# Two Mamba layers: delta spread by DMA, and centring, skip and residual as matmuls

## What is computed

```python
def _mamba_block(seq, ...):                      # seq (b, L, 96), L = 4096
    mu = seq.mean(-1, keepdims=True)
    var = ((seq - mu) ** 2).mean(-1, keepdims=True)
    h = (seq - mu) * jax.lax.rsqrt(var + EPS) * ln_g + ln_b
    xz = h @ in_w
    xs, z = jnp.split(xz, 2, axis=-1)            # 192 channels each
    xp = jnp.pad(xs, ((0, 0), (DCONV - 1, 0), (0, 0)))
    xc = sum((conv_w[:, k] * xp[:, k:k + L, :] for k in range(DCONV))) + conv_b
    xc = jax.nn.silu(xc)
    dbl = xc @ xproj_w                           # dt (6), Bm (16), Cm (16)
    delta = jax.nn.softplus(dt @ dt_w + dt_b)
    dA = jnp.exp(delta[..., None] * A)
    dBx = delta[..., None] * Bm[:, :, None, :] * xc[..., None]
    hstates = scan over L of h = dA * h + dBx    # 16 states per channel
    y = jnp.einsum('blds,bls->bld', hstates, Cm) + Dp * xc
    y = y * jax.nn.silu(z)
    return y @ out_w
seq = seq + _mamba_block(seq, ...)               # twice
```

## Time and profile before

| | |
|---|---|
| median of three runs | 9348.97 us |
| the profiled execution | 9345.01 us, span from first to last instruction 9342.9 us |
| PE (TensorE) busy | 7302.2 us, 78% |
| DVE (VectorE) | 6834.6 us, 73% |
| POOL (GpSimd) | 5443.5 us, 58% |
| ACT (ScalarE) | 4997.8 us, 53% |
| granted TensorE clock, mean | 0.857 of full |
| DMA, all on SyncE's hardware queue | 698 MB, 30.7% of 16 engines' span |

### The profile page before, as it was taken

How to read it: one execution, slowest core, us unless ns; L and a number is a source line. 1 busy time by engine, 2 the same in 40 slices (tenths; PEclk the granted TensorE clock), 3 DMA queues, 4 the chain that set the end, 5 groups by cost and what they waited for, 6 DMA issues and landing times. The chain is left out here.

```text
span 9342.9 us, 107667 instructions
## 1 busy us (share of the span) xinstructions
PE 7302.2 (78%) x19376; PEld 2489.5 (27%) x19376; DVE 6834.6 (73%) x7955; ACT 4997.8 (53%) x10430; POOL 5443.5 (58%) x4360
## 2 busy tenths in 40 slices
PE   7777777767777777288888888788888886888877
PEld 2222222222222222022222222222222221445433
DVE  6877878858878788558888899388888895532445
ACT  5555555545555555345566666455666664321456
POOL 5666666656666666147777778377777784000325
PEclk8888888878888888689999999889999998996688
DMA  2222222212222222423333343233333343165322
GB/s 52 48 47 47 47 47 47 46 42 49 51 49 51 48 48 45 118 70 79 83 85 85 85 92 86 59 81 82 89 89 89 91 95 82 78 210 162 100 55 76
DMA packets 367705, 698.09 MB, mean 75 GB/s; under 512 B 41415, under 2 KB 109372, under 8 KB 362364
## 3 DMA queue, kind: packets, MB, share of 16 engines
q1 hardware_dynamic: 367420, 695.26, 30.7%
HBM read 568.49 MB, written 126.63 MB: 74 GB/s over the span
## 5 line engine op out<-in xcount | busy, mean ns | idle before, releaser
L591 POOL TENSOR_TENSOR mamba_prod<-mamba_hs,mamba_BC_rep 128x512 f32<-128x512 f32 x1536 | 1935.1, 1267 | 1123.5 <-DVE mamba_hs L533 1113.6
L533 DVE TENSOR_TENSOR_SCAN mamba_hs<-mamba_dA,mamba_carry,mamba_dbx 128x512 f32<-128x512 f32 x1152 | 1464.4, 1271 | 130.1 <-ACT mamba_dA L462 123.4
L462 ACT ACTIVATE mamba_dA<-mamba_delta_rep,mamba_a_neg 128x512 f32<-128x512 f32 x1536 | 1036.9, 679 | 846.7 <-PE mamba_delta_rep L293 795.7
L1539 POOL TENSOR_TENSOR scan_a_prod<-scan_a_hs,scan_a_BC_rep 128x512 f32<-128x512 f32 x768 | 979.2, 1275 | 479.5 <-DVE scan_a_hs L1465 381.6
L1539 POOL TENSOR_TENSOR scan_b_prod<-scan_b_hs,scan_b_BC_rep 128x512 f32<-128x512 f32 x768 | 979.3, 1275 | 469.0 <-DVE scan_b_hs L1465 373.4
L293 PE MATMUL mamba_delta_rep<-mamba_du,mamba_sel 96*128 96x512 f32 x768 | 529.8, 778 | 653.4 <-ACT mamba_dA L462 653.3
L507 DVE TENSOR_TENSOR mamba_dbx<-mamba_u_rep,mamba_BC_rep 128x512 f32<-128x512 f32 x1152 | 790.2, 686 | 111.5 <-PE mamba_u_rep L293 56.9
L1846 POOL TENSOR_TENSOR ffn_sq<-ffn_xm 96x512 f32<-96x512 f32 x64 | 66.2, 1035 | 1156.5 <-DVE ffn_xm L1814 1145.7
L293 PE MATMUL mamba_u_rep<-mamba_du,mamba_sel 96*128 96x512 f32 x768 | 494.3, 731 | 234.8 <-DVE mamba_hs L533 155.4
L256 PE MATMUL mamba_pre<-mamba_h,mamba_w_conv 96*96 96x512 f32 x1024 | 611.0, 719 | 18.7 <-POOL mamba_tails L561 13.4
L1311 ACT ACTIVATE scan_a_dA<-scan_a_delta_rep,scan_a_a_neg 128x512 f32<-128x512 f32 x768 | 518.4, 678 | 156.7 <-PE scan_a_delta_rep L1098 143.5
(11 more groups left out here) (365 smaller groups left out, 14212.3 us busy)
## 6 DMA issues: line engine op xcount, KB each, us to landing
mamba_BC_rep<-bc_units SPq DMA_DIRECT2D x256, 512.0 KB, 9.4
scan_a_BC_rep<-bc_rows SPq DMA_DIRECT2D x512, 256.0 KB, 5.0
scan_b_BC_rep<-bc_rows SPq DMA_DIRECT2D x512, 256.0 KB, 4.8
by_n<-fin_res SPq DMA_DIRECT2D x32, 768.0 KB, 3.3
fmid_src<-by_n SPq DMA_DIRECT2D x32, 768.0 KB, 6.2
by_k<-fmid_res SPq DMA_DIRECT2D x32, 768.0 KB, 4.3
fout_src<-by_k SPq DMA_DIRECT2D x32, 768.0 KB, 4.7
seq<-mamba_xo SPq DMA_DIRECT2D x64, 192.0 KB, 2.1
```

What stands on the lines that cost most here:

```text
L462: nc.scalar.activation(dA[:, s % RING_A], delta_rep[:], ACT.Exp, scale=a_neg[:, s:s + 1]).then_inc(s_dA, 1)
L533: nc.vector.tensor_tensor_scan(hs[:, s % RING_H], dA[:, s % RING_A], dbx_bank(s)[:], carry[:, bass.ds(at, 1)], op0=ALU.mult, op1=ALU.add). ...
L591: pool.tensor_tensor(prod[:, (G * u + s) % RING_P], hs[:, s % RING_H], BC_rep[:, u, QUADS + s % QUADS], ALU.mult).then_inc(s_prod, 1)
L1539: pool.tensor_tensor(prod[:, (G * k + s) % RING_P], hs[:, (G * k + s) % RING_H], BC_rep[:, k, 2 + s % 2], ALU.mult).then_inc(s_prod, 1)
```

## The change

Delta is no longer spread by matmuls: each softplus half of 96 x 512 is stored to HBM (`delta_rows`), and read back in four loads of 192 KB (32 partitions x 3 blocks x 512 tokens) into `delta_rep`, now a tile in SBUF for two units (`spread_delta`, called for half 0 and half 1 ahead of `spread_bc` on SyncE's queue). dA waits for it in steps 0 and 12. The bank that this frees takes the output sum `out_ps`. Centring is one matmul with (identity - 1/96); ScalarE copies the result (`xm`) and squares it. The skip is a matmul of xc with a diagonal matrix that opens the sums in `y`, the residual one with the identity that opens `out_ps`; ScalarE evicts `out_ps` in its step 14 (`evict_out`). The gate moves from GpSimd to VectorE and reads `y` in PSUM; it stands where `add_skip` stood. Further: RING_H 6 to 8, RING_A 4 to 6, the projection in steps 10 and 11, softplus in ScalarE's steps 15 to 17, `copy_bc` in step 17 (was 12), `add_softplus` in steps 13 and 14, `project_out` in steps 7 and 8, buffers reused in place, softplus's halves with semaphores of their own.

The diff, with declarations, setup and context cut:

```diff
-    RING_H = 6
-    RING_A = 4
+    RING_H = 8
+    RING_A = 6
...
-        sp_abs = p.sb("sp_abs", [C, 2, T])
-        sp_exp = p.sb("sp_exp", [C, 2, T])
...
-        du = p.sb("du", [C, 2, 2, 2, T])
+        delta = p.sb("delta", [C, 2, T])
+        du = p.sb("du", [C, 2, 2, T])
+        delta_rep = p.sb("delta_rep", [128, 2, BLOCKS, T])
...
-        dA = p.sb("dA", [128, 4, T])
+        dA = p.sb("dA", [128, RING_A, T])
...
-        yg = p.sb("yg", [C, 2, T])
...
-        delta_rep = p.ps("delta_rep")
+        out_ps = p.ps("out_ps", (C, T))
...
+            def spread_delta(v, half, done, landed):
+
+                sp.wait_ge(s_delta[half], done)
+                sp.dma_start(delta_rows[v, half], delta[:, half]).then_inc(s_delta_out[half], 16)
+                sp.wait_ge(s_delta_out[half], landed)
+                by_block = delta_rows[v, half].rearrange("(b c) t -> c b t", c=32)
+                for k in range(NB):
+                    sp.dma_start(delta_rep[32 * k:32 * k + 32, v, HB * half:HB * half + HB], by_block
+                                 ).then_inc(s_rep_d[half], 16)
...
             def body(n, u, has_next, has_ahead):
...
                 if not (isinstance(n, int) and n + 3 >= UNITS):
-                    wait(sp, s_xm, read)
...
                                  ).then_inc(s_xin[1 - u], 16)
-                wait(sp, s_xo, last)
+                wait(sp, s_out, last)
...
+                    spread_delta(1 - u, 0, done, landed)
+                    spread_delta(1 - u, 1, done, landed)
...
-            sp.wait_ge(s_xm, 1)
...
+            spread_delta(0, 0, 1, 16)
+            spread_delta(0, 1, 1, 16)
...
+            pe.wait_ge(s_diag, 3)
...
             def mean(m, v):
...
-                nc.tensor.matmul(pre[0][0:C], mean_w[:], xin[:, v], start=True, stop=True).then_inc(s_mean, 1)
+                nc.tensor.matmul(pre[0][0:C], centre_w[:], xin[:, v], start=True, stop=True).then_inc(s_mean, 1)
...
             def project(m, v, half, has_ahead=False):
...
-                if half == 0:
-                    wait(pe, s_xo, m - 1)
-                elif has_ahead:
+                if half and has_ahead:
...
-            def project_out(n, kh):
-                if kh == 0 and isinstance(n, int) and n == UNITS - 1:
-                    pe.wait_ge(s_xo, n)
-                elif kh == 0 and isinstance(n, int) and n == UNITS - 2:
-                    pe.wait_ge(s_relu, 2 * n + 3)
-                elif kh == 0:
-                    pe.wait_ge(s_raw, 4 * n + 11)
+            def project_out(n, u, kh):
+                if kh == 0:
+                    wait(pe, s_xo, n)
+                    pe.wait_ge(s_xres[u], 16 * (n // 2 + 1) if isinstance(n, int) else 8 * (n - u) + 16)
+                    nc.tensor.matmul(out_ps[:], ident[:], xres[:, u], start=True, stop=False)
                 pe.wait_ge(s_yg, 2 * n + kh + 1)
-                mm = nc.tensor.matmul(pre[1][0:C], w_out[:, kh], yg[:, kh], start=(kh == 0), stop=(kh == 1))
+                mm = nc.tensor.matmul(out_ps[:], w_out[:, kh], ysk[:, kh], start=False, stop=(kh == 1))
...
-            def replicate(bank, v, what, b):
-
-                return nc.tensor.matmul(bank[:], sel[:, b % HB], du[:, v, what, b // HB], start=True, stop=True)
-
-            def rep_delta(v, b):
-                replicate(delta_rep, v, 0, b).then_inc(s_rep_d, 1)
...
             def rep_input(v, b):
-                replicate(u_rep[b % 2], v, 1, b).then_inc(s_rep_u, 1)
+                nc.tensor.matmul(u_rep[b % 2][:], sel[:, b % HB], du[:, v, b // HB], start=True, stop=True
+                                 ).then_inc(s_rep_u, 1)
...
             def sum_quad(n, u, half, i):
...
                 if i == 0:
-                    wait(pe, s_ysk, 2 * n + half)
+                    wait(pe, s_yg, 2 * n + half)
+                    nc.tensor.matmul(y[:], skip_w[:, half], xc[:, u, half], start=True, stop=False)
...
                                             prod[:, (G * u + HG * half + QUADS * c + i) % RING_P],
-                                            start=(i == 0), stop=(i == QUADS - 1))
+                                            start=False, stop=(i == QUADS - 1))
...
             def next_step(s, m, v, has_ahead):
-                if 8 <= s < 10:
-                    project(m, v, s - 8, has_ahead)
+                if 10 <= s < 12:
+                    project(m, v, s - 10, has_ahead)
...
             def ahead_step(s, m, v):
-                if s == 1:
+                if s == 2:
                     mean(m, v)
-                elif s == 5:
+                elif s == 6:
...
             def body(n, u, has_next, has_ahead):
                 for s in range(G):
                     b = s // QUADS
-                    if s % QUADS == 1 and (b + 1 < BLOCKS or has_next):
-                        if b + 1 == BLOCKS:
-                            pe.wait_ge(s_du, 3 * n + 5)
-                        pe.wait_ge(s_dA, G * n + QUADS * (b + 1))
-                        rep_delta(u if b + 1 < BLOCKS else 1 - u, (b + 1) % BLOCKS)
...
                         if b + 2 == BLOCKS:
-                            pe.wait_ge(s_du, 3 * n + 6)
+                            pe.wait_ge(s_du, n + 2)
...
                         next_step(s, n + 1, 1 - u, has_ahead)
-                    if s in (4, 6) and not (isinstance(n, int) and n == 0):
-                        project_out(n - 1, (s - 4) // 2)
+                    if s in (7, 8) and not (isinstance(n, int) and n == 0):
+                        project_out(n - 1, 1 - u, s - 7)
...
+            for half in range(2):
+                nc.scalar.activation(skip_w[:, half], ident[:], ACT.Copy, scale=skip[:, half:half + 1]).then_inc(s_diag, 1)
...
             def rsqrt(m):
...
-                nc.scalar.activation(lnv[:], pre[0][0:C], ACT.Ln, bias=eps[:]).then_inc(s_ln, 1)
+                wait(act, s_xh, m)
+                nc.scalar.activation(rstd[:], pre[0][0:C], ACT.Ln, bias=eps[:]).then_inc(s_ln, 1)
...
-                wait(act, s_xh, m)
-                nc.scalar.activation(rstd[:], lnv[:], ACT.Exp, scale=-0.5).then_inc(s_rstd, 1)
+                nc.scalar.activation(rstd[:], rstd[:], ACT.Exp, scale=-0.5).then_inc(s_rstd, 1)
...
             def softplus_begin(m, half):
...
-                wait(act, s_du, 3 * m)
-                nc.scalar.activation(sp_abs[:, half], pre[1 - half][0:C], ACT.Abs, bias=dt_b[:, half:half + 1]
+                wait(act, s_delta[half], m)
+                nc.scalar.activation(sp_ln[:, half], pre[1 - half][0:C], ACT.Abs, bias=dt_b[:, half:half + 1]
...
             def softplus_end(m, half):
...
-                nc.scalar.activation(sp_exp[:, half], sp_abs[:, half], ACT.Exp, scale=-1.0).then_inc(s_spe, 1)
+                nc.scalar.activation(sp_ln[:, half], sp_ln[:, half], ACT.Exp, scale=-1.0).then_inc(s_spe, 1)
...
-                nc.scalar.activation(sp_ln[:, half], sp_exp[:, half], ACT.Ln, bias=1.0).then_inc(s_sp, 1)
+                nc.scalar.activation(sp_ln[:, half], sp_ln[:, half], ACT.Ln, bias=1.0).then_inc(s_sp, 1)
...
             def square(m):
-                act.wait_ge(s_xm, m + 1)
+                act.wait_ge(s_mean, m + 1)
                 wait(act, s_var, m)
-                nc.scalar.activation(sq[:], xm[:], ACT.Square).then_inc(s_sq, 1)
+                wait(act, s_xh, m)
+                nc.scalar.activation(xm[:], pre[0][0:C], ACT.Copy).then_inc(s_xm, 1)
+                nc.scalar.activation(sq[:], pre[0][0:C], ACT.Square).then_inc(s_sq, 1)
+
+            def evict_out(n):
+                act.wait_ge(s_out, n + 1)
+                wait(act, s_store, 16 * n)
+                nc.scalar.activation(xo[:], out_ps[:], ACT.Copy).then_inc(s_xo, 1)
...
             def next_step(s, m, v):
-                if s < 3 and not (s == 0 and isinstance(m, int) and m == 1):
-                    to_raw(m, s + 1)
-                elif s == 6:
+                if 2 <= s < 5 and not (s == 2 and isinstance(m, int) and m == 1):
+                    to_raw(m, s - 1)
+                elif s == 10:
                     silus(m, v)
-                elif 10 <= s < 12:
-                    softplus_begin(m, s - 10)
-                elif s == 12:
+                elif s == 15:
+                    softplus_begin(m, 0)
+                elif s == 16:
+                    softplus_end(m, 0)
+                    softplus_begin(m, 1)
+                elif s == 17:
+                    softplus_end(m, 1)
                     copy_bc(m)
-                elif 13 <= s < 15:
-                    softplus_end(m, s - 13)
...
             def ahead_step(s, m):
-                if s == 3:
+                if s == 8:
                     square(m)
-                elif s == 8:
+                elif s == 11:
                     rsqrt(m)
-                elif s == 15:
+                elif s == 14:
                     affine(m)
-                elif s == 21:
+                elif s == 22:
...
             def body(n, u, has_next, has_ahead):
```

(69 more changed lines are left out.)

32 lines of the change are left out of this document (17 added, 15 removed).

## The result

The changed kernel takes 9506.4 us (median of four runs, 9506.16 to 9507.16) against 9349.9 of the kernel before on the same chip: a ratio of 1.0169, 95% interval 1.0152 to 1.0187. It is slower by 156 us, or 1.7%; 9519 was predicted. The profiled execution has a span of 9504.4 us.

A forecast was written before the change was run, and what follows sets the result against it. VectorE's order of work was taken to bound the kernel; with B and C queued behind delta, units go from 57.2 to 59.6 us: +149, first units +25, last units -4, about +170 on 9345.0, median 4 above: 9519 us (range 9290 to 9720).

## What to carry to other kernels

Work moved from an engine to DMA is to be judged less by its traffic than by its place in the queue: list what stands behind the new transfers, and who waits for that. Here the ten transfers cost 15.8 us per unit when they were put ahead of B and C in the kernel before, and by the waits left some 1.2 at most in the changed one once B and C went first and were made two steps sooner. Before such a change, ask which of the queue's customers has the shortest slack, and take the time of a load from loads as near to its size as the trace has.

## What the runs showed of the hardware

- The same four loads of 512 KB take 12.7 us from one HBM buffer and 15.1 from another 64 KB behind it (changed kernel, medians of 31 units each); with one buffer all take 12.7. That the place decides is shown by two kernels; why it does is not.
- A store of 192 KB lands 2.1 us after its issue when alone and 3.9 behind four loads on its queue, 0.3 after the last of them (medians). A store of 64 KB on ScalarE's queue, issued in the midst of the same loads, took 3.2 us in the median, and in 54 of 57 units it was there before the last of them, by 1.8 in the median.
- At the first product behind the end of a loop VectorE stands once more; in the changed kernel the profile names nothing that it waits for:

```profile
1025.07 0.70 DVE L518 TENSOR_TENSOR mamba_dbx<-mamba_u_rep,mamba_BC_rep 128x512 f32<-128x512 f32 x1 [11.56 <-DMA mamba_BC_rep<-bc_units]
...
1028.52 0.70 DVE L518 TENSOR_TENSOR mamba_dbx<-mamba_u_rep,mamba_BC_rep 128x512 f32<-128x512 f32 x1 [1.57 <-issue]
```

The loop runs over two units and turns back 24 times in the two phases; the waits are these 24, 40 us. It is not the long stall that brings them. Every kernel here has 24 waits at this product and none at the same product elsewhere, under one name or another: 15 us in all in the kernel before, 57 with B and C first, 30 with them early, 43 with the rings undone, where VectorE hardly ever waits for B and C. Without delta's transfers, where the stall is 3 us, they are 40 us as in the changed kernel, most of them put down to `u_rep`:

```profile
DVE mamba_dbx L514 <- PE mamba_u_rep L302: 36.5, 22, 1.8
...
DVE mamba_dbx L514 <- issue: 3.2, 2, 1.6
```

What sets their length is open.
- dA read from SBUF takes 712 ns, from PSUM it took 679 (both in the groups of the whole run). The Trainium skill, "Perfetto Trace Analysis", section "Optimizing Scalar/DVE Operations", gives ScalarE an overhead of some 93 ns on SBUF and 51 on PSUM, 42 apart; the rows show 33. ScalarE is busy for 55% of the changed kernel's first window, and VectorE never waits for dA there.

The group rows of dA in the kernel before and in the changed kernel:

```profile
L462 ACT ACTIVATE mamba_dA<-mamba_delta_rep,mamba_a_neg 128x512 f32<-128x512 f32 x1536 | 1036.9, 679 | 846.7 <-PE mamba_delta_rep L293 795.7 <-DVE mamba_hs L533 48.8
```

```profile
L475 ACT ACTIVATE mamba_dA<-mamba_delta_rep,mamba_a_neg 128x512 f32<-128x512 f32 x1536 | 1091.7, 712 | 285.9 <-DVE mamba_hs L537 268.2
```
